# Two of sixteen input products of a state space scan go from VectorE to ScalarE and TensorE

## The reference, cut to what matters

```
xc = silu(conv(x_in) + conv_b);  xdbl = xc @ W_xproj        # dt_r, B (16 columns), C (16 columns)
dt = softplus(dt_r @ W_dt + b_dt);  A = -exp(A_log)          # 256 channels x 16 states
h_t = h_{t-1} * exp(dt_t * A) + dt_t * B_t * u_t              # u = xc
y_t = sum over the 16 states of h_t * C_t
out = x + ((y + xc * D_param) * silu(z)) @ W_out
```

## Time and profile before

| | |
|---|---|
| Median of 3 runs | 1828.63 us (1827.78 to 1828.71) |
| Profiled execution | 1827.04 us, span 1825.3 us |
| Busy share of the span | PE 80%, PEld 54%, DVE 77%, ACT 48%, POOL 49% |
| State space stage | about 700 to 1206 us of the span |
| VectorE scans, line 1734 | 256, 297.0 us busy |
| VectorE input products, line 1728 | 256, 162.7 us busy |
| GpSimd products with C, line 1564 | 128, 299.8 us busy |
| TensorE sums of y, line 1813 | 512, 269.5 us busy |

### The profile page before, as it was taken

How to read it: one execution, slowest core, us unless ns; L and a number is a source line. 1 busy time by engine, 2 the same in 40 slices (tenths; PEclk the granted TensorE clock), 3 DMA queues, 4 the chain that set the end, 5 groups by cost and what they waited for, 6 DMA issues and landing times. The chain is left out here.

```text
span 1825.3 us, 29645 instructions
## 1 busy us (share of the span) xinstructions
PE 1469.1 (80%) x9963; PEld 991.7 (54%) x9963; DVE 1412.3 (77%) x2910; ACT 875.2 (48%) x1352; POOL 895.2 (49%) x790
## 2 busy tenths in 40 slices
PE   8988987999789996878877887768898821599990
PEld 4554555988656663333333333336777611499990
DVE  6999985879658878989999999957778767644445
ACT  3555543566545545666566656426565511022225
POOL 4455541444501013777887788645353300367753
PEclk8999997999989998989999999979999965699995
DMA  5000000000000003444443444420000050377755
GB/s 151 2 0 0 0 1 18 12 1 2 1 12 1 0 1 105 139 124 144 132 148 129 140 134 144 148 88 9 6 9 5 2 158 0 115 253 236 241 179 143
DMA packets 86430, 142.94 MB, mean 78 GB/s; under 512 B 13258, under 2 KB 39154, under 8 KB 85794
## 3 DMA queue, kind: packets, MB, share of 16 engines
q1 hardware_dynamic: 80898, 131.71, 22.7%
q0 software_dynamic: 4544, 9.32, 1.4%
q10 hardware_dynamic: 864, 0.33, 0.1%
HBM read 129.31 MB, written 12.00 MB: 77 GB/s over the span
## 5 line engine op out<-in xcount | busy, mean ns | idle before, releaser
L1813 PE MATMUL PS<-m_hC,identf 128*128 128x512 f32 x512 | 269.5, 660 | 92.1 <-POOL m_hC L1564 91.8
L1564 POOL TENSOR_TENSOR m_hC<-m_h,m_Cs 128x1024 f32<-128x1024 f32 x128 | 299.8, 2355 | 88.1 <-DVE m_h L1734 69.3
L1734 DVE TENSOR_TENSOR_SCAN m_h<-m_dA,PS 128x512 f32<-128x512 f32 x256 | 297.0, 1201 | 0.0
L1813 PEld LDWEIGHTS PS<-m_hC,identf 128*128 128x128 f32 x512 | 98.9, 205 | 237.3 <-POOL m_hC L1564 135.4
L1678 ACT ACTIVATE m_dA<-m_DT,m_A 128x508 f32<-128x508 f32 x256 | 167.6, 711 | 41.3 <-DVE m_h L1734 29.6
L1728 DVE TENSOR_TENSOR PS<-PS,m_Bs 128x512 f32<-128x512 f32 x256 | 162.7, 681 | 2.4 <-ACT PS L1669 2.4
L2277 PE MATMUL PS<-e_xT,e_WT 128*128 128x128 f32 x1136 | 139.7, 277 | 0.0
L2277 PEld LDWEIGHTS PS<-e_xT,e_WT 128*128 128x128 f32 x1136 | 133.8, 194 | 0.0
L1967 POOL DMA_INDIRECT e_XG<-token_rows,e_ids x71 | 68.8, 969 | 132.1 <-DVE e_ids L2179 110.8
L2028 ACT ACTIVATE e_Sg<-PS 128x512 f32<-128x512 f32 x71 | 42.4, 597 | 188.8 <-PE PS L2277 188.8
L2192 DVE TENSOR_TENSOR e_HT<-PS,e_Sg 128x512 f32<-128x512 f32 x71 | 49.1, 692 | 100.8 <-PE PS L2277 100.8
(11 more groups left out here) (405 smaller groups left out, 3545.4 us busy)
## 6 DMA issues: line engine op xcount, KB each, us to landing
e_WT<-in_w_wgu SPq DMA_DIRECT2D x71, 512.0 KB, 3.6
m_Bs<-state_rows SPq DMA_DIRECT2D x128, 256.0 KB, 3.2
m_Cs<-state_rows SPq DMA_DIRECT2D x128, 256.0 KB, 3.5
token_rows<-X SPq DMA_DIRECT2D x2, 2048.0 KB
e_Y<-expert_rows SPq DMA_DIRECT2D x16, 256.0 KB, 3.8
k_BD<-in_w_bcr SPq DMA_DIRECT2D x1, 2464.0 KB, 8.7
e_w_wd<-in_w_wd SPq DMA_DIRECT2D x1, 2048.0 KB, 7.9
out_dram<-X SPq DMA_DIRECT2D x8, 256.0 KB, 2.3
```

Of the source, the lines that this page charges most:

```text
L1564: nc.gpsimd.tensor_tensor(hC[:, G % NY], hst[:, G % NH], wide(Cs[:, G % RB, :]), ALU.mult).then_inc(s["hC"], 1)
L1734: nc.vector.tensor_tensor_scan(hst[:, G % NH, ch, :], dA[:, G % NA, ch].rearrange("p b l -> p (b l)"), bank(DBU + ch), 0.0, ALU.mult, ALU. ...
L1813: ins = nc.tensor.matmul(bank(YB + ch), c.identf[:, :], hC[:, G % NY, ch, :], start=False, stop=(n == NS - 1))
```

## The change

In groups 1 to 7 the steps n = 11 and n = 15 (`TURNED`) get their input product in another way. TensorE turns dt x u to token-major (`tokens`), ScalarE copies it to `DUT` (`tokens_copied`). TensorE also turns B's 16 rows (`b_tokens`), and ScalarE copies them to `BT` (`b_copied`), so that B is one number per partition. For a turned step ScalarE scales `DUT` by that number in four pieces of 128 x 256 into `E2` (`scaled`), and TensorE turns the result back with eight transposes into the PSUM banks `DBU` (`turn`), which the scan reads. VectorE skips its two products in these steps, and SyncE skips the rows of B. The due times of many stages are moved by a step or two; `x3` now stands behind step 15. `turn` has the due time G - 2.9 on TensorE, `scaled` G + 1.55 on ScalarE.

```diff
-    OWN = {... "xn_copy": -16.6, "x0": -20.5, "x1": -19.5, "x2": -18.5, "x3": -17.5,
-           "silus": -13.6, "dt_b_c": -15.5, "parts": -11.6, "dt0": -13.5, "dt1": -13.4, "dt_bias": -9.6, "exps": -8.5, "logs": -7.5,
-           "corrected0": -10.5, "corrected1": -8.5, "softplus": -6.5, "inputs": -4.5, "z0": -8.5, "z1": -7.5, "z_copy0": -3.4, "z_copy1": -2.4,
-           "staged": 1.5, "gate": 17.5, "output0": 21.6, "output1": 22.6, "stats": 25.5, "rstd": 25.6, "norm": 30.5, "silu_z": 16.5}
+    OWN = {... "xn_copy": -18.1, "x0": -20.9, "x1": -19.5, "x2": -17.5, "x3": -16.4,
+           "silus": -12.6, "dt_b_c": -14.5, "parts": -10.6, "dt0": -12.5, "dt1": -12.4, "dt_bias": -8.6, "exps": -7.5, "logs": -6.5,
+           "corrected0": -9.5, "corrected1": -7.9, "softplus": -6.4, "inputs": -4.6, "z0": -9.1, "z1": -8.1, "z_copy0": -5.1, "z_copy1": -4.1,
+           "staged": 1.5, "gate": 17.5, "output0": 23.6, "output1": 24.6, "stats": 27.5, "rstd": 27.6, "norm": 31.5, "silu_z": 16.5,
+           "bt": -10.9, "bt_copy": -6.4, "tokens0": 5.5, "tokens1": 6.5, "tokens_copy0": 9.6, "tokens_copy1": 10.6}
     EARLY = {0: {...
-                 "output0": 20.6, "output1": 21.6, "stats": 23.5, "rstd": 23.6, "norm": 28.5},
+                 "output0": 23.6, "output1": 24.6, "stats": 26.5, "rstd": 26.6, "norm": 30.2},
...
+    TURNED = (11, 15)
+    turned = lambda G: G >= NS and G % NS in TURNED
+    by_rows = [G for G in range(NG * NS) if not turned(G)]
...
+            def scaled(g, n):
+                k = len(TURNED) * (g - 1) + TURNED.index(n)
+                act.wait_ge(s["tc"], CH * g)
+                act.wait_ge(s["btc"], g)
+                act.wait_ge(s["dBu"], CH * (g * NS + n - 1))
+                if n == TURNED[0] and g + 1 < NG:
+                    act.wait_ge(s["t"], 2 * g + 1)
+                for b in range(GB):
+                    ins = nc.scalar.activation(E2.rearrange("p c (b l) -> p (c b) l", b=GB)[:, CH * b:CH * b + CH, :], DUT[:, b], ACT.Copy, scale=BT[:, g % 2, b, n:n + 1])
+                ins.then_inc(s["sc"], 1)
...
             def step(g, n):
                 G = g * NS + n
-                for ch in range(CH):
+                for ch in range(0 if turned(G) else CH):
...
+            def tokens(ch):    
+                def stage(g, par):
+                    pe.wait_ge(s["du"], g)
+                    if ch == 0:
+                        pe.wait_ge(s["ab"], CH * min(g + 2, NG))
+                        if g >= 2:
+                            pe.wait_ge(s["x"], g - 1)
+                    else:
+                        pe.wait_ge(s["tc"], CH * (g - 1) + 1)
+                    for b in range(GB):
+                        ins = nc.tensor.transpose(PS[:, 7, b * P:(b + 1) * P], DU[:, ch, b * P:(b + 1) * P], c.identf[:, :])
+                    ins.then_inc(s["dut"], 1)
+                return stage
+
+            def turn(g, n):    , due G - 2.9
+                G = g * NS + n
+                pe.wait_ge(s["sc"], len(TURNED) * (g - 1) + TURNED.index(n) + 1)
+                for ch in range(CH):
+                    pe.wait_ge(s["h"], CH * (G - 1) + ch + 1)
+                    for b in range(GB):
+                        ins = nc.tensor.transpose(PS[:, DBU + ch, b * P:(b + 1) * P], E2.rearrange("p c (b l) -> p (c b) l", b=GB)[:, CH * b + ch, :], c.identf[:, :])
+                    ins.then_inc(s["dBu"], 1)
```

More of the change, by code:

```diff
@@ L1423, in state_space @@
     twice, Dp = sb("twice", [P, P]), sb("Dp", [P, CH, P])
+    DUT, BT = sb("DUT", [P, GB, CH, P]), sb("BT", [P, 2, GB, NS])
     dA = sb("dA", [P, NA, CH, GB, P])
@@ L1452, in state_space, with run @@
     LATE = 2
     STORE = [16] + [g * NS + 11 for g in range(1, NG - 1)]
-    LATER = ("corrected0", "corrected1", "softplus", "inputs", "staged")
+    LATER = ("corrected0", "corrected1", "softplus", "inputs", "staged", "bt", "bt_copy", "tokens0", "tokens1", "tokens_copy0", "tokens_copy1")
+    TURNED = (11, 15)
+    turned = lambda G: G >= NS and G % NS in TURNED
+    by_rows = [G for G in range(NG * NS) if not turned(G)]
     def aux(g, ch):
         return bank((1 if g == 0 else 7, 0)[ch])
-    def run(setup, step, stages):
+    def run(setup, step, stages, turn=None, ahead=0.0):
@@ L1464, in run @@
         setup()
         due = [(G, step, G // NS, G % NS) for G in range(NG * NS)]
+        if turn is not None:
+            due += [(G + ahead, turn, G // NS, G % NS) for G in range(NG * NS) if turned(G)]
         for name, stage in stages.items():
@@ L1486, in store @@
                 if g >= 2:
-                    for ready in bs + cr:
-                        sp.wait_ge(ready, 16 * (g - 1) * NS // RB)
+                    for i in range(RB):
+                        sp.wait_ge(bs[i], 16 * len([at for at, G in enumerate(by_rows) if at % RB == i and G < (g - 1) * NS]))
+                        sp.wait_ge(cr[i], 16 * (g - 1) * NS // RB)
                 sp.dma_start(c.BCD[g % 2], xd[0:32, :]).then_inc(s["bcs"], 16)
@@ L1662, in logs, with b_copied, tokens_copied @@
                     nc.scalar.activation(E2[:, :, :], E2[:, :, :], ACT.Copy, bias=-1.0).then_inc(s["c1"], 1)
+            def b_copied(g, par):
+                act.wait_ge(s["bt"], g)
+                if g >= 3:
+                    act.wait_ge(s["sc"], len(TURNED) * (g - 2))
+                nc.scalar.copy(BT[:, par].rearrange("p b n -> p (b n)"), PS[:, 0, 0:GB * NS]).then_inc(s["btc"], 1)
+            def tokens_copied(ch):
+                def stage(g, par):
+                    act.wait_ge(s["dut"], CH * (g - 1) + ch + 1)
+                    if g >= 2:
+                        act.wait_ge(s["sc"], len(TURNED) * (g - 1))
+                    nc.scalar.copy(DUT[:, :, ch, :], bl(bank(7))).then_inc(s["tc"], 1)
+                return stage
[9 more added lines that the diff above has]
+                ins.then_inc(s["sc"], 1)
             def staged(g, par):
@@ L1686, in _ @@
             stages = {"inner_norm": inner_norm, "xn_copy": normalised, "silus": silus, "parts": parts, "dt_bias": step_sizes, "exps": exps, "logs": logs,
-                      "z_copy0": z_copied(0), "z_copy1": z_copied(1), "staged": staged, "silu_z": last_gates, "norm": norm}
+                      "z_copy0": z_copied(0), "z_copy1": z_copied(1), "staged": staged,
+                      "bt_copy": b_copied, "tokens_copy0": tokens_copied(0), "tokens_copy1": tokens_copied(1), "silu_z": last_gates, "norm": norm}
             setup()
             routed_act(act, opening(stages), OPEN)
-            run(lambda: None, step, stages)
+            run(lambda: None, step, stages, scaled, 1.55)
         @block.vector
@@ L1771, in stage @@
                         pe.wait_ge(s["ab"], g * CH + CH)
+                        if g:
+                            pe.wait_ge(s["btc"], g)
                     else:
@@ L1802, in step_sizes, with b_tokens, stage, turn @@
                 return stage
+            def b_tokens(g, par):
+                pe.wait_ge(s["ab"], g * CH + CH)
+                for b in range(GB):
+                    ins = nc.tensor.transpose(PS[:, 0, b * NS:(b + 1) * NS], xd[0:NS, b * P:(b + 1) * P], c.identf[0:NS, 0:NS])
+                ins.then_inc(s["bt"], 1)
+            def tokens(ch):
+                def stage(g, par):
+                    pe.wait_ge(s["du"], g)
+                    if ch == 0:
+                        pe.wait_ge(s["ab"], CH * min(g + 2, NG))
+                        if g >= 2:
+                            pe.wait_ge(s["x"], g - 1)
[4 more added lines that the diff above has]
+                    ins.then_inc(s["dut"], 1)
+                return stage
+            def turn(g, n):
+                G = g * NS + n
+                pe.wait_ge(s["sc"], len(TURNED) * (g - 1) + TURNED.index(n) + 1)
+                for ch in range(CH):
+                    pe.wait_ge(s["h"], CH * (G - 1) + ch + 1)
+                    for b in range(GB):
+                        ins = nc.tensor.transpose(PS[:, DBU + ch, b * P:(b + 1) * P], E2.rearrange("p c (b l) -> p (c b) l", b=GB)[:, CH * b + ch, :], c.identf[:, :])
+                    ins.then_inc(s["dBu"], 1)
             def step(g, n):
@@ L1831, in _ @@
             stages = {"xn_T": transposed, "x0": project_x(1, 0), "x1": project_x(1, 1), "x2": project_x(0, 0), "x3": project_x(0, 1), "dt_b_c": dt_b_c,
-                      "dt0": step_sizes(0), "dt1": step_sizes(1), "z0": project_z(0), "z1": project_z(1), "output0": output(0), "output1": output(1)}
+                      "dt0": step_sizes(0), "dt1": step_sizes(1), "z0": project_z(0), "z1": project_z(1),
+                      "bt": b_tokens, "tokens0": tokens(0), "tokens1": tokens(1), "output0": output(0), "output1": output(1)}
             pe.wait_ge(wsem, wcount)
             routed_pe(pe, opening(stages), OPEN)
-            run(setup, step, stages)
+            run(setup, step, stages, turn, -2.9)
             keep_warm(c, 12, 1)
```

29 lines of the change are left out of this document (18 added, 11 removed).

## The result

The changed kernel takes 1842.0 us (median of 6 runs, 1839.9 to 1846.3) against 1828.9 for the kernel before on the same chip: a ratio of 1.0069, with a 95% interval of 1.0054 to 1.0084. It is slower by 0.7%, clear of the spread. The forecast of 1831.3 has the right sign and is 10.7 us short.

The account below looks back on a forecast made before the run. VectorE bounds the group (busy 58.3 of 61.8 us). Per group 5.7 saved, 6.0 lost, +0.35; groups 2 to 5 +1.4, 7 -2.4, 6 +0.4, 0 +0.9, 1 +2.3: +2.6, median 1831.3; own range 1826 to 1838, overall 1815 to 1843.

Parts of the forecast that it names:

- The stall before step 11: Sign of being right: VectorE idles some 6 us before step 11's first scan in groups 2 to 5.
- the gate waits: Sign of being right: VectorE's waits of 2.76 us before the gate fall below 0.5.
- group 7: It prepares no next group, so GpSimd isn't late: its interval shrinks by 2.4 us.
- the sign given for being wrong: Gate intervals of 56 to 59 us, or above 63 with TensorE at half its clock beyond step 7.
- The chain of step 11: GpSimd's late step 7 delays TensorE, z's copy, pieces and turn: scan 11 at 39.15, VectorE idle 6.0 us per group.
- The 3.33 us of waits: Per group, moving conv part and statistics removes VectorE's waits of 2.76 before the gate and 0.57 before output statistics.
- the half output, 1.4: TensorE's half output after step 7's matmuls, before z's second product and step 11's turn, takes 1.4 us.
- the second rival: The low clock lasts: half output and z product take 2.2 us more in groups 1 to 6; 1844, chance 0.22.
- the turn of step 15 is nearly in time: GpSimd recovers during the stall before step 11, so step 15 adds little; about 0.2 us for the second turn.
- The sum: Groups 2 to 5 +1.4, group 7 -2.4, group 6 +0.4, group 0 +0.9, group 1 +2.3: +2.6 us.
- The last one: ScalarE's work is on the path in full: 1.7 replaces 1.18 us per turned step, 7.3 slower, 1836; chance 0.06.
- The first rival: Turned steps come nearly in time: groups 1 to 5 gain 3.0 more each, group 6 about 2; 1814, chance 0.29.

Follow-up runs that it names:

- second and third experiment: Changed kernel with 18 constant matmuls added on TensorE in groups 2 to 5, 1830.8 us; changed kernel with GpSimd's corrected0, corrected1, softplus one step later, 1823.5 us.
- the third experiment: Changed kernel with GpSimd's corrected0, corrected1 and softplus one step later, behind one more product with C: 1823.5 us, ratio 0.996.
- the fifth experiment: Changed kernel, all in time: GpSimd's corrected0, corrected1, softplus and inputs later, stages of output, norm and z moved to fit: 1800.0 us, ratio 0.9841.

## Why the prediction was right in part

**By its own signs.** The stall before step 11 (5.9 to 7.3 us in groups 2 to 5), the gate waits, GpSimd's start and group 7 came near the forecast. Two signs of being right failed in groups 3 to 5: VectorE idles 1.3 to 1.4 before step 15, where under 1 was stated, and the intervals are 64.65 to 64.76. Intervals above 63 with TensorE at half its clock beyond step 7 were the sign given for being wrong, and in these groups they came. The measured 1842.0 also lies outside the forecast's own range of 1826 to 1838. It is inside 1815 to 1843 by 1 us, and only because that range makes room for the rivals.

**The chain of step 11 held, step by step.** In group 4, from the gate: the `- 1` ended at 22.7 (forecast 22.5), `corrected0` began at 22.7 (22.6), the product of step 7 ran from 26.85 to 29.2 (26.7 to 29.1), its matmuls took 3.57 (3.45), the pieces 1.69 (1.7), and VectorE was free at 33.2 (33.1). The pieces did stand behind z's second copy and the exponentials of step 12. The gate and statistics waits went in groups 2 to 5. In group 2 the whole sum holds: idle 5.90 (forecast 6.0), interval 62.23 (62.15).
```profile
883.00 2.33 DVE L1774 TENSOR_TENSOR_SCAN m_h<-m_dA,PS 128x512 f32<-128x512 f32 x2 [5.90 <-PE PS L1873]
```
One term came out right for another reason than the one given. The 3.33 us of waits counted as removed by the spread stay when the parts are only spread (3.20). In the changed kernel the wait of the statistics goes because a longer stall stands ahead of it.

**The first mis-sized term: the half output, 1.4.** It took 2.40 in group 4 (2.30 and 2.49 in groups 3 and 5), because the low clock lasted beyond step 7, and 2.2 in group 6, where I expected no low clock at all. That is the second rival in part: it had 2.2 more for half output and z's product, and the clock came back by z's second product (1006.02), so that 1.0 came. In group 2 the same 4.37 us of idling led to the same slow step 7, but then to a half output of 1.34:
```profile
873.17 3.44 PE L1885 MATMUL PS<-m_hC,identf 128*128 128x512 f32 x4 [4.37 <-POOL m_hC L1574]
876.45 0.39 PE L1898 MATMUL PS<-X,m_twice 128*128 128x128 f32 x2
...
877.79 1.02 PE L1816 MATMUL PS<-m_xnT,w_win 128*128 128x512 f32 x2
```
There the clock was full again (1.00 from 876.45 to 877.79). I had read the recovery from one row of before and taken it for all groups. With 0.2 to 0.3 of small differences it makes scan 11 start at 40.44 instead of 39.15.

**The second: "the turn of step 15 is nearly in time", 0.2.** It cost 1.34. GpSimd's `inputs` and four small operations of the norm stand ahead of step 12's product; TensorE idles 2.01, and step 12 and the turn run at the low clock (3.00 and 1.38 where 1.72 and 0.93 stand at full clock). I had assumed that GpSimd recovers during the stall.

**The sum.** Groups 3 to 5 lose 2.9 instead of 0.35 (7.6 more in all), group 6 3.1 instead of 0.4 (2.7 more: step 15's wait of 1.37, and a low clock in step 7 and the half output after 2.59 us of idling, where I had expected none), group 1 3.5 instead of 2.3 (the statistics wait 11.05 there, at 820.67, ahead of the scan). Together 11.5 of the 11.7 us by which the sum was short; groups 0, 2 and 7 were right. The 1.2 of group 1 are not a fixed cost: the two runs of the second and third experiment leave that group's code as it is, and it takes 62.62 and 62.54 there instead of 64.10.

**The rivals.** The last one, that the swap costs in full what ScalarE takes for it, falls by the third experiment. The second one's 1844 is near the measured 1842.0, but by luck: it put 2.2 more on each of groups 1 to 6 for the clock, and none came in group 2 and 1.0 in group 4. The waits before step 15, 5.4 us in all, which it didn't have, made up for much of that. The Trainium skill, "ScalarE: Activation LUTs", section "Rules for kernel authors", gives multiplication to VectorE; here, once in time, the turned steps on ScalarE made 1800.0 of 1806.9 (some 4 us of it in the stage), so on this kernel the rule does not decide. The first rival (turned steps in time, 1814) did not come in the changed kernel; the due times of the fifth experiment give it, and more.

## What to carry to other kernels

Taking work off the bounding engine did not pay here while what replaced it was queued, in another engine's order, behind something late for a different reason; before costing such a swap, follow the order on that engine back to the first wait of its own. A wait that a longer stall covers is not gone, it is back when the stall goes (2.80 before the statistics with only step 15 turned), so edits have to be judged together: spreading the parts and GpSimd's new order are worth some 3.7 us each alone and 23 together with the stages fitted to them. And a recovery of the clock, read from one place, should be a range in the sum.

## What the runs showed of the hardware

How long TensorE stays at the low clock after idling is not fixed by the idle time alone. After 4.37 and 4.38 us in the same kernel the clock was full by 3.28 us of work in group 2 and still 0.50 up to 5.45 us in group 4 (the stretch 1004.05 to 1005.50 above):
```profile
876.45:877.79 1.34, 1.34 (x14) 1.34 (x12) 0.65 (x1) 0.00 (x0) 1.34 (x2) 1.00 0.49 135
```
An idle time of 2.01 was followed by the low clock in the changed kernel (1022.30). So was one of 2.23 before step 11 in the third experiment, whose matmuls then took 3.51 at a granted clock of 0.51. One of 2.25 before the same step in the run with all in time was not, and there they took 1.82 at full clock:
```profile
1011.00 3.68 PE L1885 MATMUL PS<-m_hC,identf 128*128 128x512 f32 x4 [2.23 <-POOL m_hC L1574]
```
```profile
992.86 1.98 PE L1885 MATMUL PS<-m_hC,identf 128*128 128x512 f32 x4 [2.25 <-POOL m_hC L1574]
```
What decides it, these runs don't show.
